# First attention: the value copies go to ScalarE, the value bias is added to the products of probabilities and values on VectorE

## The reference, cut to what matters

```
x = x + attention(layernorm(x), W_Q, W_K, W_V, W_O, b_Q, b_K, b_V, b_O)

q = einsum('bpd,hde->bphe', x, W_Q) + b_Q      # k, v likewise with b_K, b_V
scores = einsum('bqhe,bkhe->bhqk', q, k) / ATTN_SCALE
scores = where(causal, scores, IGNORE)
attn = softmax(scores, axis=-1)
z = einsum('bkhe,bhqk->bqhe', v, attn)
out = einsum('bqhe,hed->bqd', z, W_O) + b_O
```

## Time and profile before

| | us |
|---|---|
| median of 3 runs | 1829.67 |
| the profiled execution | 1836.18 |
| its span, first to last instruction | 1834.4 |
| PE busy | 1622.0 |
| DVE busy | 1131.4 |
| ACT busy | 972.8 |

### The profile page before, as it was taken

How to read it: one execution, slowest core, us unless ns; L and a number is a source line. 1 busy time by engine, 2 the same in 40 slices (tenths; PEclk the granted TensorE clock), 3 DMA queues, 4 the chain that set the end, 5 groups by cost and what they waited for, 6 DMA issues and landing times. The chain is left out here.

```text
span 1834.4 us, 25838 instructions
## 1 busy us (share of the span) xinstructions
PE 1622.0 (88%) x8598; PEld 1300.2 (71%) x8598; DVE 1131.4 (62%) x2496; ACT 972.8 (53%) x2789; POOL 538.3 (29%) x447
## 2 busy tenths in 40 slices
PE   6999989989989867899999759998889999999866
PEld 5878877767877656667777637777667888788634
DVE  4654576677558676444443455554347778767878
ACT  4644544445444553223223535687747666666756
POOL 2224232743353172311002364445021122211000
PEclk9999999999999998899999867988789999999989
DMA  7144234522444162133434310100030111000001
GB/s 270 47 144 144 98 106 143 211 98 98 135 146 149 48 172 64 58 104 121 128 107 126 125 46 21 35 4 24 1 135 19 42 40 33 13 1 1 1 1 47
DMA packets 87511, 151.50 MB, mean 83 GB/s; under 512 B 9940, under 2 KB 45396, under 8 KB 87380
## 3 DMA queue, kind: packets, MB, share of 16 engines
q1 hardware_dynamic: 81236, 133.07, 22.2%
q0 software_dynamic: 6144, 16.79, 2.9%
HBM read 90.84 MB, written 58.98 MB: 82 GB/s over the span
## 5 line engine op out<-in xcount | busy, mean ns | idle before, releaser
L790 PE MATMUL bank<-self_attention 128*128 128x256 f32 x512 | 128.9, 397 | 27.0 <-DVE residual L1672 17.9
L2594 ACT ACTIVATE cross_attention_heads<-cross_attention_heads,small 128x128 f32<-128x128 f32 x256 | 99.6, 390 | 89.3 <-DVE small L2029 89.3
L2338 ACT ACTIVATE self_attention<-self_attention,small 128x128 f32<-128x128 f32 x256 | 99.9, 392 | 84.8 <-DVE small L1658 83.5
L1126 PE MATMUL bank<-cross_attention,cross_attention_heads 128*128 128x256 f32 x512 | 125.0, 387 | 15.3 <-DVE residual L2043 10.1
L790 PEld LDWEIGHTS bank<-self_attention 128*128 128x128 f32 x512 | 98.9, 197 | 47.6 <-DVE residual L1672 24.1
L595 PE MATMUL bank<-x_channel_major,qkv_weights_split 128*128 128x512 f32 x256 | 119.0, 465 | 6.4 <-DVE qkv_weights_split L1690 2.9
L1126 PEld LDWEIGHTS bank<-cross_attention,cross_attention_heads 128*128 128x128 f32 x512 | 95.9, 192 | 38.9 <-DVE residual L2043 19.0
L2506 ACT ACTIVATE narrow_late<-bank,small 128x128 f32<-128x128 f32 x256 | 91.3, 377 | 58.7 <-DVE small L1900 58.2
L2698 POOL CAST qkv_weights_split<-self_attention 128x1024 fp32r<-128x1024 f32 x45 | 50.4, 1120 | 234.4 <-DMA self_attention<-in_wqkv 205.8
L2700 POOL TENSOR_TENSOR qkv_weights_split<-self_attention,qkv_weights_split 128x1024 fp32r<-128x1024 f32 x45 | 109.3, 2430 | 3.6
L888 PE MATMUL bank<-experts,tiles 128*128 x316 | 108.0, 465 | 0.4 <-DVE tiles L1778 0.4
(11 more groups left out here) (398 smaller groups left out, 4724.3 us busy)
## 6 DMA issues: line engine op xcount, KB each, us to landing
picked_inputs<-self_attention SPq DMA_DIRECT2D x64, 512.0 KB
self_attention<-in_wqkv SPq DMA_DIRECT2D x48, 512.0 KB
experts_far<-picked_inputs SPq DMA_DIRECT2D x79, 128.0 KB, 2.1
picked_outputs<-tiles SPq DMA_DIRECT2D x79, 128.0 KB, 1.7
self_attention<-in_wo SPq DMA_DIRECT2D x16, 512.0 KB
experts<-in_moe SPq DMA_DIRECT2D x4, 1408.0 KB
self_attention<-in_bv SPq DMA_DIRECT2D x16, 256.0 KB, 5.1
context_values<-context_out SPq DMA_DIRECT2D x16, 256.0 KB
```

Of the source, the lines that this page charges most:

```text
L790: m = T.matmul(bank[7][:, 0:D], ZT_a[n % 2][:, h, :], wo_a[p % 2][:, h, :], start=h == 0, stop=h == HG - 1)
L1126: m = T.matmul(bank[7][:, 0:D], ZT_x[n % 2][:, h, :], x_wo[hg % 2][:, h, :], start=h == 0, stop=h == HG - 1)
L2338: m = S.activation(P_a[u][:, h, :], P_a[u][:, h, :], ACT.Exp, bias=negmax_a[u][:, h:h + 1], accum_out=sums_a[u][:, h:h + 1])
L2594: m = S.activation(P_x[u][:, h, :], P_x[u][:, h, :], ACT.Exp, bias=negmax_x[u][:, h:h + 1], accum_out=sums_x[u][:, h:h + 1])
```

## The change

Values are taken out of PSUM by ACT as a plain copy, without the bias, in the place where ACT's fill had nothing to do. DVE takes over the copy of the products of values and probabilities and adds the bias there. In that tile a head's channel is the partition, so the bias is one column for each head: `bv_columns`, 128x16. It is made once: a DMA of 16x128, a transpose on PE into bank 7 after the first twelve fills, and a copy of 128x16 on ACT. The 16 DMAs of `bv_a` are gone, and SP's wait for `v_out` ahead of them. DVE's step is now values(n-3), output(n-4), norm(n-1), scores(n), five side pieces.

```
         # tensor, after the fills of pass 0
+            pe.wait_ge(got_bv, 16)
+            T.transpose(bank[7][:, 0:H], bv_rows[0:H, :], ident[0:H, 0:H]).then_inc(bv_turned, 1)
         # vector
-            def fill(p, i):
-                if i >= 8:
-                    n = GB * p + i - 8
-                    dve.wait_ge(fill_done, 12 * p + i + 1)
-                    dve.wait_ge(a_values, n - NV + 1)
-                    dve.wait_ge(got_bv_a[p % 2], 16 * (p // 2 + 1))
-                    V.tensor_tensor(v_a[n % NV], bank[(12 * p + i) % 2][:, :], bv_a[p % 2], ALU.add).then_inc(v_out, 1)
+            def values(n):
+                heads_at = n // GB % NHG * HG
+                dve.wait_ge(a_values, n + 1)
+                dve.wait_ge(a_output, n - 1)
+                dve.wait_ge(bqs_set, 2)
+                V.tensor_tensor(ZT_a[n % 2], four(bank[6][:, :]),
+                                bv_columns[:, heads_at:heads_at + HG].unsqueeze(2).broadcast_to([P, HG, P]), ALU.add).then_inc(a_Z, 1)
...
+                if 3 <= n < NSTEP + 3:
+                    values(n - 3)
                 if n >= 4:
                     output(n - 4)
...
-                side.step(3)
-                if more:
-                    fill(p + 1, 3 * b)
-                side.step()
-                if more:
-                    fill(p + 1, 3 * b + 1)
-                side.step()
-                if more:
-                    fill(p + 1, 3 * b + 2)
+                side.step(5)
         # scalar
+                else:
+                    n = GB * p + i - 8
+                    act.wait_ge(fill_done, 12 * p + i + 1)
+                    act.wait_ge(a_values, n - NV + 1)
+                    S.copy(v_a[n % NV], bank[(12 * p + i) % 2][:, :]).then_inc(v_out, 1)
...
-            def values(n):
-                act.wait_ge(a_values, n + 1)
-                act.wait_ge(a_output, n - 1)
-                S.copy(ZT_a[n % 2], four(bank[6][:, :])).then_inc(a_Z, 1)
...
+            act.wait_ge(bv_turned, 1)
+            S.copy(bv_columns, bank[7][:, 0:H]).then_inc(bqs_set, 1)
...
-                if 3 <= n < NSTEP + 3:
-                    values(n - 3)
         # sync
-                sp.wait_ge(v_out, GB * (p - 1))
-                D_(bv_a[p % 2], io["bv0"][hg * HG * DH:(hg + 1) * HG * DH].partition_broadcast(P)).then_inc(got_bv_a[p % 2], 16)
...
+            D_(bv_rows[0:H, :], io["bv0"].rearrange("(h d) -> h d", d=DH)).then_inc(got_bv, 16)
```

More of the change, by code:

```diff
@@ L295, in build @@
         ZT_a = [four(ar.take(512)) for _ in range(2)]
-        bv_a = [ar.take(HG * DH) for _ in range(2)]
+        bv_rows = ar.take(DH)
         causal = ar.take(P)
@@ L300, in build @@
         negmax_a, sums_a, rinv_a = ([sm.take(HG) for _ in range(3)] for _ in range(3))
-        bqs = sm.take(H)
+        bqs, bv_columns = sm.take(H), sm.take(H)
         right = ExitStack()
@@ L470, in build @@
         got_wo_a = [semaphore(f"got_wo_a{s}") for s in range(2)]
-        got_bv_a = [semaphore(f"got_bv_a{s}") for s in range(2)]
+        got_bv, bv_turned = semaphore("got_bv"), semaphore("bv_turned")
         got_causal, got_bo_a, got_router = semaphore("got_causal"), semaphore("got_bo_a"), semaphore("got_router")
@@ L509, in build @@
         c_proj, c_key, c_v = Again(fill_done, 12 * NHG * NG), Again(v_out, NSTEP), Again(wkv_exps, 2 * KT * NG)
-        c_squared, c_root = Again(route_exps, NG), Again(bqs_set, 1)
+        c_squared, c_root = Again(route_exps, NG), Again(bqs_set, 2)
         n_bo_hi_set, n_bo_lo_set = Again(n_w_hi, KT), Again(n_w_lo, KT)
@@ L514, in build @@
         v_stored = [Again(sem, 16 * NHG * NG // 2) for sem in got_wo_a]
-        got_v = [Again(sem, 16 * NHG * NG // 2) for sem in got_bv_a] + [Again(sem, 16 * 3 * NHG * NG // 2) for sem in got_wqkv]
+        got_v = [Again(sem, 16) for sem in (got_bv, got_router)] + [Again(sem, 16 * 3 * NHG * NG // 2) for sem in got_wqkv]
         cross_filled, cross_read = semaphore("cross_filled"), semaphore("cross_read")
         got_wq, got_wo_x, got_mask = semaphore("got_wq"), [semaphore(f"got_wo_x{s}") for s in range(2)], semaphore("got_mask")
-        x_bias_turned, x_bias_set = semaphore("x_bias_turned"), semaphore("x_bias_set")
+        x_bias_turned, x_bias_set = Again(bv_turned, 1), semaphore("x_bias_set")
         x_w_lo, x_fill, x_taken, x_qturned, x_q, x_squared, x_summed, x_root, x_inverse = (
@@ L1082, in turn_bias @@
                     m = T.transpose(bank[1][:, h * P:(h + 1) * P], vec[:, c:c + 1].broadcast_to([P, P]), ident[:, :])
-                m.then_inc(x_bias_turned, 1)
+                m.then_inc(x_bias_turned.sem, 1)
             def turn_queries(f):
@@ L1690, in vector_program @@
                 V.tensor_tensor(wqkv[m][1], third(m), wqkv[m][0].bitcast(F32), ALU.subtract).then_inc(w_first, 1)
-            for i in range(12):
-                fill(0, i)
             for n in range(NSTEP + 4):
-                p, b = divmod(n, GB)
-                more = p + 1 < NHG * NG
                 if n == 0:
```

## The result

| | kernel before | changed kernel |
|---|---|---|
| median of 15 runs each, same chip | 1832.9 us (1825.15 to 1839.33) | 1839.0 us (1831.36 to 1848.98) |
| ratio | 1 | 1.0035, 95% interval 1.0019 to 1.0050 |
| profiled execution / span | 1836.18 / 1834.4 us | 1843.96 / 1842.2 us |

What follows compares the result with a forecast made beforehand. PE, busy 88% of the span, was taken to bound the kernel through its gaps and clock; terms of -11.1, -6.6, -7.9, -2.0, -6, +3.0, +1.5, +1.8 summed to -27.3 us, from 1829.67 to 1802.4 us, range 1791 to 1820.

Steps and rivals of the forecast that it cites:

- (a): Value fills: PE's 12.0 us of waits for DVE go, 0.9 us for ACT's copies comes: -11.1 us.
- (b): Copy of the products: three of PE's five waits for ACT's copy, 8.7 us in all, go: -6.6 us.
- (c): Output: PE's 17.9 us in 9 waits for DVE's output shrink by 7.9 us; bounds -13 and +5.
- (d): Wkv recurrence piece behind value fills: two adds of 0.6 leave each of three waits, -2.0 of 3.8 us.
- -3.6 for the hold: Output at 515.52 us: PE's 5.20 us loss behind DVE's "remote" hold shrinks by 3.6 if DVE is no longer held.
- (e): Granted clock: four stretches hold 12.4 us of lost speed; half comes back, -6 us, bounds 0 and -12.
- (f): New waits: +3.0 us in three wkv stretches, +1.5 in steps 3 and 7, +1.8 in the last steps.
- +1.5 for the norms of steps 3 and 7: ACT's copies of values 10 and 11 come behind its piece of the norm, which waits for DVE's moments: +1.5 us.
- inner range of the forecast: The summed forecast with its halves for output waits and clock either way: 1795 to 1811 us.
- Rival 1: PE's gaps only move: value fills are gained, output waits grow; about -8 us, 1822 us, chance 0.12.
- Rival 2: Add ahead of the output costs 0.61 us per late step, up to +39: 1842 us; chance 0.03 with anything else slower.
- Rival 3: DVE's "remote" hold stays or lands on another tight place: about -19 us, 1811 us, chance 0.16.

Runs made afterwards that it cites:

- e4: Changed kernel with VectorE's products' add placed behind the output's add instead of ahead: 1812.5 us, ratio 0.9986 to before, 6.5 us under the changed kernel.
- e16: Changed kernel with VectorE's output add moved between the side pieces of the step ahead: 1803.64 us, ratio 0.9958 to before.
- e13: ScalarE doing both copies, no value bias, plus a spare VectorE reduce at the head of the 24 recurrence steps: ratio 1.0043 to before.

## Why the prediction was wrong, by its steps

(a) The value-fill waits on DVE went, and ScalarE's copies of values are a gain: -0.86% by themselves. But where I put 0.9 us for PE's waits on ScalarE, the first profile has 2.5 and the 5.4 by "issue" as well, which end with two copies that ScalarE made late (356.27 and 512.86 us, after 8.24 and 7.35 us of "remote").

(b) Right as a row: no wait for ScalarE's copy of the products is left. But PE's waits in front of L790 went only from 26.6 to 20.9 us together, and the operation cost more time on VectorE than it had on ScalarE.

(c) and (d) fell: -7.9 became +3.0, -2.0 became +6.8. Only the -3.6 for the hold came near: PE did the output there at once and then lost 2.50 us, which now stand under (a). At step 8 DVE's output began at 106.56 and PE still lost 4.31 us. The two adds of 0.6 that left DVE's side pieces came back in its step's head, in front of the same output and the same piece.

(e) fell short: by the same four stretches the lost clock went from 12.4 to 10.6 us in the first pair (0.91 to 0.87 from 225 to 265 us, but 0.83 to 0.91 from 95 to 115 and 0.91 to 1.00 from 500 to 520), 1.8 of the 6. In the second profiles the changed kernel's recurrence stretches have the lower clock.

(f) is the step that failed: "about 1.0 us in each of three wkv stretches, +3.0", and +1.8 for the seven last steps. Against the half without the adds, on the same chip, the adds cost 8.0 us in the recurrence's stretches, 5.7 in the last one and 4.4 between (1.3 of that a longer wait for POOL's split), 18.3 by the profiles and 21.3 by the medians. I took as cover that DVE idles a third of the stage, an average. I had seen it 30.9 of 40 us busy from 225 to 265 and filed that under a rival. 24 operations of 0.67 us in those steps cost 23 us by the ratios, 16 by the profiles; the other 23 little. No row showed the +1.5 for the norms of steps 3 and 7, and in the changed kernel's first profile PE has no wait for a value copy before 98 us.

The inner range of the forecast, 1795 to 1811, ends at 1809 by its own halves.

Rival 1 named the mechanism and then kept a gain of 8 us, since it counted the add's cost only as lost gains of (b) and (c). Rival 2 named the place, the add ahead of the output, and e4 and e16 bear it out; it asked for 45 late steps, but PE waited for the output in 12 only, and the recurrence's pieces, which it left out, did the rest. Rival 3's count of instructions fell: the holds by "remote" stayed about where they were (compare),

```profile
507.92 0.69 DVE L1666 TENSOR_TENSOR self_attention<-bank,small 128x512 f32<-128x512 f32 x1 [7.52 <-remote]
512.86 0.59 ACT L2329 COPY self_attention<-bank 128x512 f32<-128x512 f32 x1 [7.35 <-remote]
513.50 0.51 PE L595 MATMUL bank<-qkv_weights_split,x_channel_major 128*128 128x512 f32 x1 [2.50 <-issue]
513.63 0.69 DVE L1649 TENSOR_TENSOR self_attention<-bank,self_attention 128x512 f32<-128x512 f32 x1 [3.88 <-remote]
```

and another such place, at 350 to 357 us, is in both first profiles too. PE lost 2.50 us here and 2.86 there, before 5.20 and 1.9. In the second profiles of both kernels neither DVE nor ScalarE has such a hold from 31 to 645 us, though the DMA share from 500 to 520 us of before is 0.81 again. The count in blocks of 256 instructions, which the prediction took from the Trainium skill (Runtime: NRT & Kernel Launch, "Instruction fetch mechanics"), therefore named no cause that the runs bear out; what the holds are stays open. That the 24 reduces cost 23 us by the ratios and 16 by the profiles is for the most part the choice of execution: the profiled one of e13, 1812.78 us, was the fastest of its twelve, 6.5 under their median.

## What to carry to other kernels

Price an added operation by the stretch in which the waited-for engine is late, not by that engine's share over the stage: there 16 us of spare work cost 16 us or more, elsewhere 15 us of it cost 2 to 4. Moving as much work to an engine as one takes from it is not neutral when the added operation stands at the head of each step, ahead of what the bound engine needs; look first whether that needed operation can stand earlier (here it gave back 0.73 points). Cut the stage at the same step of every kernel, where the bound engine passes it, before saying in which stretch the time was lost. And when a change has two halves, forecast each by itself: here one was worth 0.86%, the other cost 1.19%.

## What the runs showed of the hardware

A VectorE multiply with two SBUF inputs took 0.69 us at its shortest and 2.82 us beside a GpSimd operation on the weights; its mean fell from 918 to 728 ns with GpSimd's split cut. The granted clock of a 200 us stretch differed between executions by enough to cover the change's effect (0.81 to 0.88 from 1090 to 1290 us in profiles of these two kernels), so one pair of profiles pointed to the wrong stage, and a second pair put it right.
